# A recommendation tower on one core: separate home for the pair weights, pair products of a tile in one run, layer 2 transposed

## What is computed

```python
e = stack([tbl_f[ids[:, f]] for f in range(27)], axis=1)          # 512 x 27 x 128, float32
pairs = einsum('bfd,bgd->bfg', e, e)[:, TRIU_I, TRIU_J]            # 512 x 351
h = concatenate([e.reshape(512, -1), pairs, dense_ctx], axis=1)    # 512 x 3823
h = maximum(h @ W_top1 + b_top1, 0)                                # 3823 x 512
h = maximum(h @ W_top2 + b_top2, 0)                                # 512 x 256
y = h @ W_top3                                                     # 256 x 1
```

## Time and profile before

| what | value |
|---|---|
| time, median of 3 runs | 189.6 us (189.15 to 190.91) |
| profiled execution: span from first to last instruction | 214.7 us |
| PE busy in it | 156.4 us (73%), 696 products |
| DVE, ACT, POOL busy | 108.6, 99.1, 112.1 us |
| granted PE clock, mean | 0.913 |
| moved by DMA | 16.65 MB |

### The profile page before, as it was taken

How to read it: one execution, slowest core, us unless ns; L and a number is a source line. 1 busy time by engine, 2 the same in 40 slices (tenths; PEclk the granted TensorE clock), 3 DMA queues, 4 the chain that set the end, 5 groups by cost and what they waited for, 6 DMA issues and landing times.

```text
span 214.7 us, 2129 instructions
## 1 busy us (share of the span) xinstructions
PE 156.4 (73%) x696; PEld 136.0 (63%) x696; DVE 108.6 (51%) x199; ACT 99.1 (46%) x187; POOL 112.1 (52%) x114
## 2 busy tenths in 40 slices
PE   0239078549847995999987999309997999997940
PEld 0027067437736894788876889308996888996630
DVE  5688245265521765866577433212586445476020
ACT  3364055054311857962588440222679344498100
POOL 5879777887773775557267577732077530000000
PEclk9999769967995899799999999955999999999997
DMA  5769998322221111333412111831011110000000
GB/s 136 240 220 293 280 256 264 110 88 83 76 82 37 37 50 40 123 110 51 25 30 60 37 49 49 34 39 37 3 37 49 37 40 2 0 2 0 0 0 0
DMA packets 10332, 16.65 MB, mean 78 GB/s; under 512 B 3936, under 2 KB 4704, under 8 KB 10268
## 3 DMA queue, kind: packets, MB, share of 16 engines
q0 software_dynamic: 3456, 7.08, 15.9%
q1 hardware_dynamic: 6865, 9.43, 15.2%
HBM read 16.50 MB, written 0.00 MB: 77 GB/s over the span
## 4 chain that ended last, share of the span: by engine, by line
PE 33%; issue 16%; ACT 13%; DVE 13%; another core or an unknown queue 13%; DMA 6%; POOL 2%; SPq 1%; ACTq 0%; DVEq 0%
PE h_ps L563 6%; PE gram_ps L584 5%; ACT e L287 4%; DVE e L412 4%; PE h_ps L564 4%; PE h_ps L565 4%; ACT w_pairs L315 3%; DVE w_lo L402 3%; ACT stage L303 3%; PE gram_ps L619 3%; DMA stage<-in_W_top 3%; DVE w_pairs L434 3%; PE h_ps L597 3%; PE tp_ps L545 2%
## 5 line engine op out<-in xcount | busy, mean ns | idle before, releaser
L266 POOL DMA_INDIRECT rows<-in_tbl,ids_sb x108 | 111.4, 1031 | 60.9 <-issue 29.1
L563 PE MATMUL h_ps<-w_hi,e 128*128 128x512 f32 x108 | 54.9, 508 | 10.4 <-DVE e L412 9.6
L412 DVE TENSOR_TENSOR e<-tp_ps,e 128x512 fp32r<-128x512 f32 (+1 forms) x28 | 31.8, 1136 | 53.3 <-issue 27.2
L287 ACT ACTIVATE e<-tp_ps 128x512 fp32r<-128x512 f32 (+1 forms) x28 | 29.4, 1050 | 54.8 <-remote 28.7
L564 PE MATMUL h_ps<-w_lo,e 128*128 128x512 f32 x108 | 46.5, 431 | 0.0
L565 PE MATMUL h_ps<-w_hi,e 128*128 128x512 f32 x108 | 46.1, 427 | 0.0
L563 PEld LDWEIGHTS h_ps<-w_hi,e 128*128 128x128 f32 x108 | 33.1, 306 | 13.6 <-DVE e L412 9.4
L545 PE MATMUL tp_ps<-ident,rows 128*128 128x128 f32 x108 | 20.9, 303 | 18.7 <-DMA rows<-in_tbl,ids_sb 18.7
L564 PEld LDWEIGHTS h_ps<-w_lo,e 128*128 128x128 f32 x108 | 34.0, 315 | 0.7
L565 PEld LDWEIGHTS h_ps<-w_hi,e 128*128 128x128 f32 x108 | 33.3, 309 | 1.5
L584 PE MATMUL gram_ps<-e 128*128 128x224 f32 x128 | 22.6, 304 | 15.3 <-DVE x_lo L415 9.2
(11 more groups left out here) (38 smaller groups left out, 86.1 us busy)
## 6 DMA issues: line engine op xcount, KB each, us to landing
stage<-in_W_top SPq DMA_DIRECT2D x14, 512.0 KB
rows<-in_tbl,ids_sb POOLq DMA_INDIRECT x108
w_pairs<-in_W_top SPq DMA_DIRECT2D x11, 28.0 KB
w_pairs<-in_W_top SPq DMA_DIRECT2D x11, 24.0 KB
stage<-in_W_top SPq DMA_DIRECT2D x1, 256.0 KB
w_pairs<-in_b_top SPq DMA_DIRECT2D x1, 128.0 KB
w_pairs<-in_W_top SPq DMA_DIRECT2D x1, 128.0 KB
w_pairs<-in_W_top SPq DMA_DIRECT2D x5, 12.0 KB
```

Of the source, the lines that this page charges most:

```text
L266: nc.gpsimd.indirect_dma_start(rows[:, n % RING, :], None, tables[f], bass.IndirectOffsetOnAxis(ids_sb[:, t, f:f + 1], 0)).then_inc(rows_l ...
L287: last = nc.scalar.activation(tile_e(0, t, fs[0], fs[-1] + 1), tp_ps[k % 2][:, 0:len(fs), :], ACT.Copy)
L412: last = nc.vector.tensor_tensor(tile_e(1, t, fs[0], fs[-1] + 1), tp_ps[k % 2][:, 0:len(fs), :], tile_e(0, t, fs[0], fs[-1] + 1), ALU.subt ...
L563: nc.tensor.matmul(out, hi, w_hi[:, f, :], start=f == 0, stop=False)
```

## The change

**Memory plan.** Every buffer has a fixed address. `e` has one buffer for all tiles instead of two. `wp` and `w_pairs` have a home of their own (the raw weights lie where the lo part will be written). The staging area grows from 10 to 16 slots, six of which lie in the area of `y`. `w2`, `b2` and `w3` have homes of their own and are loaded without a wait.

**Layers 2 and 3.** Layer 2 gives its result transposed (256 outputs in two blocks of 128 partitions, 128 samples along the row), so that bias and relu are one instruction on ACT and one on DVE, layer 3 is two products on PE with W_top3 as the fixed operand, and y is one row of 128 numbers in one partition, stored as 512 contiguous bytes. The core of the diff:

```diff
-        e = sb("e", [P, 2, 2, P, ROWS], f32r)
+        e = sb("e", [P, 2, P, ROWS], f32r)
+        wp = sb("wp", [P, 2, CI, H1], f32r)
+        w_pairs = sb("w_pairs", [P, CI, H1], f32, at=home["wp"] + 4 * CI * H1)
...
             for c in range(0, F, PER_DMA):
                 if c >= STAGE:
                     sp.wait_ge(w_lo_ready, c + n - STAGE)
-                elif c >= 4:
-                    sp.wait_ge(rows_landed[c - 4], 16)
+                if c >= 6:
+                    sp.wait_ge(rows_landed[(c - 6) % RING], 16 * ((c - 6) // RING + 1))
...
-                sp.dma_start(y_out[t * P:(t + 1) * P, :], y_col).then_inc(y_stored, 16)
+                sp.dma_start(y_out[t * P:(t + 1) * P, :].rearrange("p o -> o p"), y_row).then_inc(y_stored, 16)
...
@@ ACT, split_e @@
-                if t >= 2:
-                    act.wait_ge(e_used, k - NQ + 1)
-                    if q == 0:
-                        act.wait_ge(gram_done, GP * t)
+                if q == 0 and t >= 1:
+                    act.wait_ge(e_used, NQ * t)
+                    act.wait_ge(gram_done, GP * t)
...
@@ ACT, tiles 1 to 3 (DVE likewise) @@
+            for t in range(1, NT):
+                u = t - 1
+                sums(u, 0, GP)
+                split_e(t, 0)
+                if u >= 1:
+                    relu_h2(u - 1)
+                split_e(t, 1)
+                move_x(u, 0, 0)
+                move_x(u, 0, 1)
+                split_e(t, 2)
+                move_x(u, 1, 0)
+                move_x(u, 1, 1)
+                split_x(u)
+                split_e(t, 3)
+                if t == 1:
+                    split_wp()
+                split_e(t, 4)
+                relu_h1(u)
+                split_e(t, 5)
+                copy_h1T(u)
+                if t == NT - 1:
+                    relu_h2(u)
+                split_e(t, 6)
...
@@ PE @@
+            def layer2(t):
+                for m in range(MC):
+                    for c in range(HC):
...
+                        last = nc.tensor.matmul(h2T_ps[m], w2[:, c, m * P:(m + 1) * P], h1T[:, c, :],
+                                                start=c == 0, stop=c == HC - 1)
+                    last.then_inc(h2_done, 1)
+
+            def layer3(t):
...
+                nc.tensor.matmul(y_ps, w3[:, 0:1], h2T[:, 0, :], start=True, stop=False)
+                pe.wait_ge(h2_dve_ready, t + 1)
+                nc.tensor.matmul(y_ps, w3[:, 1:2], h2T[:, 1, :], start=False, stop=True).then_inc(y_done, 1)
+
+            def grams(t):
                 gram(t, 0)
+                gram(t, 1)
+                embeddings_h1(t, 6, 0, 1)
+                gram(t, 2)
+                embeddings_h1(t, 6, 1, 2)
+                gram(t, 3)
+                embeddings_h1(t, 6, 2)
+                gram(t, 4)
+                if t + 1 < NT:
+                    transposes(t + 1, 0)
+                gram(t, 5)
+                gram(t, 6)
+                gram(t, 7)
...
+            for t in range(1, NT):
+                u = t - 1
+                grams(u)
+                if u >= 1:
+                    layer2(u - 1)
+                transposes(t, 1)
+                embeddings_h1(t, 0)
+                if u >= 1:
+                    layer3(u - 1)
+                transposes(t, 2)
+                embeddings_h1(t, 1)
...
+                embeddings_h1(t, 4)
+                transpose_h1(u)
+                if t == NT - 1:
+                    layer2(u)
+                transposes(t, 6)
+                embeddings_h1(t, 5)
+                if t == NT - 1:
+                    layer3(u)
+            u = NT - 1
+            grams(u)
+            pairs_h1(u)
+            transpose_h1(u)
+            layer2(u)
+            layer3(u)
```

More of the change, by code:

```diff
@@ L35, in dlrm_tower @@
     ROWS = P // SPG
-    FM = F + F % 2
     NG = P // SPG
@@ L39, in dlrm_tower @@
     PG = NG // GP
+    FM = F + F % 2
+    GM = SPG * FM
     GSTEP = 256
@@ L62, in dlrm_tower, with sb @@
     with ctx:
-        def sb(name, shape, dt):
-            return ctx.enter_context(nc.sbuf_tensor(name, shape, dt))
+        sizes = [("w_hi", F * H1), ("w_lo", F * H1), ("e", 2 * P * ROWS), ("wp", 2 * CI * H1), ("x", 2 * CI * P),
+                 ("y", NG * GM), ("stage_a", STAGE_A * H1), ("w2", HC * H2), ("rows", RING * D), ("ident", P),
+                 ("ids_sb", NT * F), ("ctx_sb", NT * CTX), ("b2", 8), ("w3", 8)]
+        home, end = {}, -(-nc.sbuf_base // 32) * 32
+        for name, n in sizes:
+            home[name] = end
+            end += -(-4 * n // 32) * 32
+        def sb(name, shape, dt, at=None):
+            return nc.alloc_sbuf_tensor_at(name, shape, dt, offset=home[name] if at is None else at)
         def sem(name):
@@ L202, in dlrm_tower, with run_of @@
         NR = len(X_RUNS)
-        def run_of(t, x, run):
+        def run_of(part, run):
             partitions, c0, c1 = run
-            x = x if x is not None else x_first if t == 0 else x_later
-            return x[0:partitions, c0:c1, :]
+            return part[0:partitions, c0:c1, :]
         N_PAIR_LOADS = len(list(pair_weight_loads()))
@@ L353, in _ @@
             for q in range(NQ):
+                for c in quad_features(q):
+                    split_w(c)
                 split_e(0, q)
-            sums(0, 0, 2)
-            split_e(1, 0)
-            sums(0, 2, 5)
-            split_e(1, 1)
-            move_x(0, 0, 0)
-            sums(0, 5, 6)
-            split_e(1, 2)
-            move_x(0, 0, 1)
-            sums(0, 6, 8)
-            split_e(1, 3)
-            move_x(0, 1, 0)
-            move_x(0, 1, 1)
-            split_x(0)
-            split_wp()
@@ L398, in _ @@
+            u = NT - 1
+            sums(u, 0, 5)
+            move_x(u, 0, 0)
+            sums(u, 5, 6)
+            move_x(u, 0, 1)
+            sums(u, 6, 8)
+            move_x(u, 1, 0)
+            move_x(u, 1, 1)
+            split_x(u)
+            relu_h1(u)
+            copy_h1T(u)
+            relu_h2(u)
         @block.vector
@@ L530, in _ @@
-            copy_h1T(NT - 1)
-            finish_y(NT - 1)
+            nc.vector.memset(x_full, 0.0).then_inc(x_zeroed, 1)
+            for t in range(1, NT):
+                u = t - 1
+                sums(u, 0, GP)
+                split_e(t, 0)
+                if u >= 1:
+                    relu_h2(u - 1)
+                split_e(t, 1)
+                if u >= 1:
+                    copy_y(u - 1)
+                move_x(u, 0, 2)
+                move_x(u, 0, 3)
+                split_e(t, 2)
+                move_x(u, 1, 2)
+                move_x(u, 1, 3)
+                split_x(u)
+                split_e(t, 3)
+                if t == 1:
+                    split_wp()
+                split_e(t, 4)
+                split_e(t, 5)
+                copy_h1T(u)
+                if t == NT - 1:
+                    relu_h2(u)
+                    copy_y(u)
+                split_e(t, 6)
@@ L533, in _, with transposes @@
+            u = NT - 1
+            sums(u, 0, 5)
+            move_x(u, 0, 2)
+            sums(u, 5, 6)
+            move_x(u, 0, 3)
+            sums(u, 6, 8)
+            move_x(u, 1, 2)
+            move_x(u, 1, 3)
+            split_x(u)
+            copy_h1T(u)
+            relu_h2(u)
+            copy_y(u)
         @block.tensor
         def _(pe):
-            def transposes(t, q, first=0, end=QF):
+            def transposes(t, q):
                 k = t * NQ + q
@@ L539, in transposes @@
                     pe.wait_ge(ident_ready, 1)
-                if k >= 2 and first == 0:
+                if k >= 2:
                     pe.wait_ge(e_lo_ready, k - 1)
-                for i, f in list(enumerate(quad_features(q)))[first:end]:
+                for i, f in enumerate(quad_features(q)):
                     n = t * F + f
@@ L587, in gram, with pairs_h1 @@
                 last.then_inc(gram_done, 1)
-            def pairs_h1(t):
-                for c in range(CI):
-                    for i, (_, first, _) in enumerate(X_RUNS):
-                        if c == first:
+            def pairs_h1(t, first=0, end=CI):
+                for c in range(first, end):
+                    for i, (_, start, _) in enumerate(X_RUNS):
+                        if c == start:
                             pe.wait_ge(x_lo_ready, NR * t + i + 1)
```

372 lines of the change are left out of this document (119 added, 253 removed).

## The result

The changed kernel takes **200.2 us** (median of 4 runs, 198.6 to 201.1) against 189.6: ratio 1.055 [1.049, 1.062]. It is slower, by 10.6 us where 6.0 were forecast. The forecast's sign and its largest term, the tail, hold; the gain at the start did not come, and the slow clock, which stood among the rivals for the tail alone, came ahead of the first gram and at the boundary of tile 1 as well.

What follows compares the result with a forecast made beforehand. The prediction took PE to bound the kernel from the first gram on. Its terms summed to +7.2 us, less 1.2 for overlap, giving +6.0 on 189.6: 195.6 us, range 187 to 201.

Steps and rivals of the forecast that it cites:

- What bounds the kernel: From the first gram on PE binds; four stalls belong to the profiled execution, without them and their half clock span 186 us.
- The start, -3.8: Up to tile 0's gram: with W_top1 loaded alone, gathers run freer and the gram starts at 45.5, not 49.3 us.
- Gather of tile 1, +1.2: Tile 1: pair transfers fall on its gather, so PE waits 2.9 us for rows where before this cost 1.7.
- Gram in one run, +5.9: Tiles 0 to 2: PE waits on ACT and DVE between gram parts, 1.95 us idle in each tile.
- the old order's idle 6.9 us: Between grams: PE's idle time under the old order disappears, credited as -5.1 us.
- Boundary of tile 1, +3.7: Tile 1's start: PE waits for splits behind the gram's parts, 2.6 us, and 1.1 more at the fourth quad.
- End of tile 2, +1.8: Before tile 3's gram: DVE's last split waits behind the copy of y, 1.5 us, plus 0.3 for layer 2.
- Tail, +7.4: Tile 3: eleven features, 7.8 us, stand before the gram's chain instead of hidden in it; chain 0.4 shorter.
- The first rival: Tail: PE's 6.9 us wait also halves the clock, costing 2.5 us; chance 0.22 shared with slow gather or store.
- Layers 2 and 3, +0.4: Layer 2 taken as equal, layer 3 adds 0.5 us in three tiles, tail slightly longer, less 1.5 credit.
- The credit of 1.5 for fewer changes on PE: PE changes between gram and features at five places less per tile, about 0.1 us each: -1.5.
- Store, -4.3: Kernel's end: y stored in one piece, issue to end 2.4 us or a little more instead of 7.0.

Runs made afterwards that it cites:

- b_lastrow: Kernel before, only the last tile's y turned into a row and stored in one piece: 211.9 us against 218.4 in a stalled call; repeated without stalls 185.7 us.
- a_pairs: Changed kernel with one more wait on SP, so pair transfers start only when tile 0's last row has landed: 208.6 us, ratio 1.096.
- b_again: Kernel before, unchanged, profiled once more: 188.7 us, span 186.9, no stalls.
- a_wlight: Changed kernel, each W_top1 transfer from the ninth feature on bringing only 16 of 128 partitions: 227.5 us in a stalled call, ratio 1.041.
- a_copyy: Changed kernel, in tile 3 the copy of y on DVE placed behind the last split: 200.1 us, ratio 1.048.
- b_run3: Kernel before, only tile 3's gram in one run, eleven features moved ahead of it: 199.0 us, ratio 1.052.
- a_tail: Changed kernel, 7 features of tile 3 in and behind its gram run instead of 3: 198.3 us median, profiled run 196.9.
- a_both: Changed kernel with both edits: tile 3's 7 features between and behind the gram's parts, copy of y behind the last split: 198.6 us, ratio 1.048.
- b_yrow: Kernel before with transposed layer 2, layer 3 on PE and y stored as a row; loads, gram order and tail as before: 186.8 us, ratio 0.985.

## Why the prediction was right in sign and short in size

The profiles differ by 12.3 us where the sum said 6.0. Step by step:

**What bounds the kernel: right.** 49.8 against the 49.3 worked out, span 186.9 against 186. That the stalls belonged to that one execution was wrong, as b_lastrow shows, without effect on the sum.

**The start, -3.8, came out at +0.5: the step that failed, 4.3 us.** I had set the issue of row 26 at 36.5 to 38 and its landing 2.5 us later. POOL and PE in the changed kernel:

```profile
35.86 3.14 POOL L251 DMA_INDIRECT rows<-in_tbl,ids_sb  x1 [0.30 <-issue]
39.31 0.94 POOL L251 DMA_INDIRECT rows<-in_tbl,ids_sb  x1 [0.30 <-issue]
```

```profile
44.41 1.03 PE L495 MATMUL tp_ps<-ident,rows 128*128 128x128 f32 x2 [1.70 <-DMA rows<-in_tbl,ids_sb]
```

Row 26 is issued at 39.3 and transposed at 45.0, the second of these two, where the forecast has it landed at 40.5. The forecast's 38 is the end of that issue and its pause; it would have begun at 36.7. So it is 2.6 late by the issues (the 27 took 4.0 us over 0.94 each, not 1.5), and takes 5.7 from there instead of 3.8. From row 26 to the gram it is then 5.3 us, near the 5.0 that the forecast allowed, but 2.0 of these are the half clock from 43.2 to 50.0: the last twelve products ahead of the gram take 5.0 us here and 3.0 in a_pairs. Rows land in a median of 4.4 us between 14 and 30, 5.4 between 30 and 45, and 2.5 from 90 on. I took the late figure for the early stretch. The Trainium skill (DMA: Bandwidth & Descriptors, section Latency and other measured facts) gives 0.2 us of memory latency on average and 2 at high load, which goes the same way; the spread of the trace's medians, 2.9 us, is larger. The argument that gathers suffer from the pair transfers between the loads holds for the landings (b_again has 6.2 us between 14 and 30) but not for the issues: with those transfers gone from there (the changed kernel), later still (a_pairs), and with W_top1 thinned out (a_wlight), single issues of 2 to 3 us remain. All of these long issues, and the two slow ones in the earlier trace rows, stand beside DVE's series of subtractions (the end of a_wlight above): I gave the traffic the blame for what goes with DVE's work. Whether an issue falls into such a series differs from execution to execution. Over all profiles the last row of tile 0 is issued at 37.7 to 44.4, in either order of transfers, and the first gram of the undisturbed ones stands at 48.8 to 53.0 (mean 50.2 in the five of the kernel before and its variants, 50.4 in the five of the changed one and its). So a single pair of profiles can't tell +0.5 from nothing, but all ten show that the 3.8 us didn't come.

**Gather of tile 1, +1.2: not seen.** PE's waits in tile 1 are for the splits, not for rows.

**Gram in one run, +5.9: too much.** The waits are 0.6 us in tile 0 and 1.1 in tiles 1 and 2, not 1.95. Against that stand the old order's idle 6.9 us, of which I let 5.1 go. Idle time up to gram 3 rose by 2.7 us where the terms said 6.3: 5.9 + 3.7 - 5.1 + 1.8 (+1.2 - 1.2).

**Boundary of tile 1, +3.7: right**, 2.33 + 1.32 = 3.65. But what follows was missing: half clock from 60.2 to 67.0, at a price of 2.6 us. The kernel before could have shown it: behind its idle 2.60 us of the earlier trace rows (81.20 to 83.80) the clock is 0.5 from 85.3 to 88.8. The prediction counted that stretch among the four in its first section, but its rival names only waits of 4.5 us and more.

**End of tile 2, +1.8: right**, 1.48 for the wait and some tenths for layer 2; a_copyy removes it.

**Tail, +7.4: right.** The 11 features moved gram 3 (7.2 in b_run3, 2.9 for four of them in a_tail). From gram 3 to the pair products it is 15.7 us, against 16.0 forecast and 16.4 before. The first rival came in part. Of 10.2 us at half clock 3.4 fall on the pair products: their 21 starts take 6.2 us instead of 4.7, 1.6 lost, and from them to the store it is 11.3 instead of 9.5. But in the changed kernel the clock had fallen before the long wait began. In a_tail and a_both, which have no waits inside the gram run, it fell 1.7 and 1.8 us into a wait of 5.60. The rival's price of 2.5 doesn't follow from its own numbers: half of 21 products at 0.20 more is 2.1. In b_run3 it was 2.7. Another slip of the prediction has no effect: 73 transfers at 0.31 us from 33 on end at 56, not 58.

**Layers 2 and 3, +0.4: too little.** Layer 2 was right. Its group over all tiles (busy us, mean ns), changed kernel and then b_again, is 2.05 us a tile against 1.97:

```profile
L573 PE MATMUL gram_ps<-stage_a,w 128*128 128x128 f32 x64 | 8.2, 281 | 1.5 <-DVE y L392 1.0 <-DVE stage_a L418 0.5
```

```profile
L619 PE MATMUL gram_ps<-stage 128*128 128x256 f32 x32 | 7.9, 391 | 1.5 <-DVE stage L452 1.5
```

But of the 13.9 us that PE is busier from the first gram to gram 3, the features are 7.8 and the half clock 2.6; 3.5 are left. Layer 3 is 2.2 of them, 0.75 a tile. The profile shows its two products as four records a tile, two for each line, where the forecast took them as two:

```profile
L583 PE MATMUL gram_ps<-stage_a,w 128*1 128x128 f32 x8 | 1.5, 272 | 0.1
```

What the other 1.3 are no run separates. The credit of 1.5 for fewer changes on PE doesn't show in the sum.

**Store, -4.3: too careful.** 7.3 to 1.4 is -5.9; I had put the one piece at 2.4 or more, by the nearest row, a load.

In sum, against the terms: start +4.3 (2.0 of it half clock), half clock +2.6 at the boundary and +1.6 in the tail, layers and the unexplained rest of PE's work +3.5 up to gram 3, idle time -3.6, store -1.6, and -0.5 for the rest of the tail. That is +6.3, the difference between 12.3 and 6.0.

## What to carry to other kernels

Where two engines form a chain at a kernel's end, whatever work of the third is still open belongs beside that chain; 7 to 8 us were lost here by moving eleven short pieces ahead of it, and the waits that they had filled came with a halved clock. When an undisturbed stretch of the trace has a figure (a landing in 2.5 us), look for the same figure in the crowded stretch before using it there. Before a long instruction is put down to traffic, look at what every other engine does from its start to its end: here the ends of DVE's series gave the answer. And take a change apart: the one good part of this one, y as a row, is worth 4 us alone in its cheapest form, for the last tile only, where nothing hides the store.

## What the runs showed that I had not expected

- A store of 128 pieces of 4 bytes takes 7.0 to 7.3 us from its issue to the end of the span, one piece of 512 bytes 1.4 to 1.5.
- A gather issue that begins while DVE subtracts with both inputs in SBUF can last until 0.8 us after the last subtraction of the series: 3.14 us beside four in a row and 4.35 beside seven, instead of 0.94.
- A wait of 2.33 us on PE went with clock 0.5 for 3.4 to 6.8 us in four stall-free profiles of kernels with the one-buffer `e`. In the fifth, a_pairs, 3.4 us of it followed waits of 0.22, 0.61 and 1.07 at that place. The stall-free profiles of the kernel before and its variants have no half clock there. In b_yrow 3.4 us of it followed a wait of 1.69, in the changed kernel 6.8 followed 1.63 and 1.70. The prediction had said that the trace did not show this near 2 us, and the earlier trace rows had 1.45 without it; the stall-free profiles show that it can follow shorter waits than the 4.5 to 8.9 of its rival, several in a row above all. The Trainium skill (TensorE: Matmul & The Clock Gate, section on oscillation) warns of the pattern, a clock that falls again behind waits; the trace agrees on the fall.
- The stalls of ACT come in whole series of runs, in all three kernels profiled in that series (up to 9.1 us each, some 25 us in all). In the kernel before and b_lastrow they stand at the same instructions. They put the before kernel at 218.4 instead of 189.6.
